# The last norm out of the mixing norm's statistics, bf16 counts, and a query bias that rides with the side information

## What the kernel must compute

```python
x = x + tanh(g_xattn[0]) * attention(layernorm(x), ctx, side)   # softmax(Q K^T / 16 + beta * side) V, 64 keys
x = x + tanh(g_ffn[0])   * experts(layernorm(x))                # a shared expert and 2 of 8 routed experts a row
x = x + tanh(g_xattn[1]) * mixing(layernorm(x), ctx)
x = x + tanh(g_ffn[1])   * (round_and_clip(layernorm(x) / step) * step @ (ternary - 1).T + bias)

def attention(n, ctx, side):
    Q = n @ Wq.T + bq; K = ctx @ Wk.T + bk; V = ctx @ Wv.T + bv
    return softmax(Q @ K.T / 16 + beta * side) @ V

def mixing(f, ctx):                                   # f: 512 x 256, ctx: 64 x 256
    h = tanh((ctx @ Ws)[None] + (f @ W)[:, None] + b)  # 512 x 64 x 256 values of tanh a sequence
    att = softmax(h @ w + mask)                        # 512 x 64
    t = att @ ctx
    return tanh(t @ Wcw) * f + tanh(t @ Wcb)           # two numbers a row: ws and bs
```

## Time and profile before

| what | us |
|---|---|
| median of 3 runs (lowest, highest) | 1095.37 (1093.33, 1097.17) |
| the profiled execution | 1098.02 |
| its span, first to last instruction | 1096.3 |
| PE, DVE, ACT, POOL busy in the span | 996.7, 748.8, 668.2, 216.5 |

### The profile page before, as it was taken

One profiled execution on the slowest core, in us unless ns is written; L12 is line 12 of the kernel. 1 busy time (PEld: TensorE's weight loads), 2 busy tenths in 40 slices (PEclk: granted clock), 3 DMA queues, 4 the chain that ended last, 5 costly groups with the idle time before them and its releaser, 6 DMA issues.

```text
span 1096.3 us, 23452 instructions
## 1 busy us (share of the span) xinstructions
PE 996.7 (91%) x8772; PEld 771.5 (70%) x8772; DVE 748.8 (68%) x2110; ACT 668.2 (61%) x966; POOL 216.5 (20%) x257
## 2 busy tenths in 40 slices
PE   6889999999999999999999999999999999966661
PEld 2568777787779999977777777777777777622220
DVE  2566788877653345644578678578588488898876
ACT  1211111111101111399999999999999999999990
POOL 1032123331250003121122121131131121310000
PEclk9859999999999999999999999999999999999895
DMA  8011101100039999876466456656665564100000
GB/s 254 25 63 58 39 30 63 44 34 15 30 104 333 336 332 341 305 246 214 160 222 229 176 197 228 202 198 204 207 217 197 186 231 155 40 16 21 1 20 19
DMA packets 114053, 164.21 MB, mean 150 GB/s; under 512 B 13235, under 2 KB 70068, under 8 KB 113940
## 3 DMA queue, kind: packets, MB, share of 16 engines
q1 hardware_dynamic: 104004, 135.57, 36.9%
q0 software_dynamic: 9936, 27.15, 6.7%
HBM read 138.69 MB, written 23.99 MB: 148 GB/s over the span
## 4 chain that ended last, share of the span: by engine, by line
PE 72%; DVE 11%; issue 7%; ACT 7%; DMA 2%; POOL 1%; SPq 0%; POOLq 0%; DVEq 0%; ACTq 0%
PE bank L1130 21%; PE bank L1313 16%; PE bank L1292 11%; PE bank L1135 6%; PE bank L1283 3%; PE bank L1172 2%; PE bank L1116 2%; PE bank L1300 2%; ACT arena L656 2%; PE bank L1187 2%; PE bank L1219 1%; PE bank L1245 1%; DMA picked<-expert_rows,found_at 1%; DVE ln_moe_stats L748 1%; DVE x L818 1%
## 5 line engine op out<-in xcount | busy, mean ns | idle before, releaser
L1130 PEld LDWEIGHTS bank<-rowsT,expert_w 128*128 128x128 f32 x2272 | 270.8, 192 | 10.3 <-issue 6.2
L1130 PE MATMUL bank<-rowsT,expert_w 128*128 128x128 f32 x2272 | 276.6, 275 | 0.5 <-DVE rowsT L938 0.5
L648 ACT ACTIVATE act<-bank 128x512 f32<-128x512 f32 x103 | 61.3, 595 | 211.9 <-PE bank L1130 115.2
L1292 PE MATMUL bank<-expert_w,act 128*128 128x256 f32 x568 | 138.6, 387 | 1.8 <-DVE rowsT L938 1.7
L573 POOL DMA_DIRECT2D expert_rows<-rows_out x71 | 42.6, 601 | 492.7 <-DVE rows_out L955 492.7
L1135 PE MATMUL bank<-normT,shared_w 128*128 128x256 f32 x512 | 126.8, 396 | 0.0
L955 DVE COPY rows_out<-bank 128x256 f32<-128x256 f32 x71 | 30.1, 425 | 141.2 <-PE bank L1292 140.5
L664 ACT ACTIVATE tanhs<-shared_w,txtT 128x512 f32<-128x512 f32 x168 | 122.0, 726 | 2.1 <-DVE shared_w L981 2.1
L1292 PEld LDWEIGHTS bank<-expert_w,act 128*128 128x128 f32 x568 | 102.2, 190 | 28.8 <-issue 15.9
L665 ACT ACTIVATE tanhs<-shared_w,txtT 128x512 f32<-128x512 f32 x168 | 122.0, 726 | 0.0
L1135 PEld LDWEIGHTS bank<-normT,shared_w 128*128 128x128 f32 x512 | 98.3, 198 | 17.3 <-issue 3.0
(11 more groups left out here) (230 smaller groups left out, 1483.8 us busy)
## 6 DMA issues: line engine op xcount, KB each, us to landing
expert_w<-in_WgT SPq DMA_DIRECT2D x71, 512.0 KB, 4.0
expert_w<-in_WuT SPq DMA_DIRECT2D x71, 512.0 KB, 5.2
expert_w<-in_WdT SPq DMA_DIRECT2D x71, 512.0 KB, 6.7
rows_in<-rows_by_expert SPq DMA_DIRECT2D x71, 128.0 KB, 5.8
expert_rows<-rows_out POOLq DMA_DIRECT2D x71, 128.0 KB, 4.3
x<-in_x SPq DMA_DIRECT2D x8, 512.0 KB, 4.2
out<-x SPq DMA_DIRECT2D x16, 256.0 KB, 2.7
score<-in_fside SPq DMA_DIRECT2D x8, 128.0 KB, 2.3
```

The lines of the kernel that those rows point to most:

```text
L648: e.activation(act[n % 2][:, :], banks[2 * (n % 2)][:, :], ACT.Tanh, scale=0.5).then_inc(s_tanh, 1)
L1130: got = e.matmul(bank[:, i * P:(i + 1) * P], w[:, at:at + P], t[:, c * P:(c + 1) * P], start=c == 0, stop=c == DC - 1)
L1292: got = e.matmul(row_bank[:, 0:D], act[n % 2][:, c * P:(c + 1) * P], w[:, at:at + D], start=c == 0, stop=c == IC - 1)
```

## The change

Three edits of the computation, and a new set of numbers for the order.

- **The last norm.** Since x' = A x + B, its mean is A mean + B and its variance A * A * var, so (x' - mean') * r' is (x - mean) * (A * r'). The kernel after takes the variance as (1 + w1) * (1 + w1) * var with w1 = g * ws * r in three small instructions (`stretch`), so `stats` and `aggr` of that norm go; `quantize` reads x and the mixing norm's mean before `apply` has run, and `apply` moves behind `quantize`. `affine` runs between POOL's power and `newton`. The two weighted sums become one of twice the width (`weigh_c`).
- **Counts.** `before`, `chosen` and a new all-ones tile are bf16.
- **Query bias.** The prologue makes `bias_q` by a weight whose 128 columns are all bq, so the bias stands in all 128 lanes, scaled; `side` adds it together with the scaling, and the product L1183 goes. `side` of the first sequence now waits for ACT's copy of `bias_q`.
- **Numbers.** `PLACES` and `LAGS` change all over; `PAIRS` goes from 2, 4, 4, 4, 4, 4, 8, 12 to 8, 4, 4, 5, 4, 4, 10, 13, which makes 166 preadd instructions of DVE's behind the last gate activation where there were 146, and 416 in all where there were 336.

```diff
-PAIRS = {0: 2, 1: 4, 2: 4, 3: 4, 4: 4, 5: 4, 6: 8, 7: 12}
+PAIRS = {0: 8, 1: 4, 2: 4, 3: 5, 4: 4, 5: 4, 6: 10, 7: 13}
-    "scalar": {"gate_act": -2.5, "soft_rho": 1, "softmax": -2, "spread": 7.5, "squash": 0.5, "tanh": 1.5, ("turn", "att"): -0.5,
+    "scalar": {"gate_act": -1, "soft_rho": 1, "softmax": -2, "spread": 7.5, "squash": -1, "tanh": 0.5, ("turn", "att"): -0.5,
...
-        return ([[("rho", b)], [], [("turn_rho", b)], [("soft_rho", b)], [("rsum", b)], [("weigh_ws", b)], [("weigh_bs", b)],
-                 [("squash", b)], [("affine", b)], [("apply", b)]] + self.norm("lin", b, False)
-                + [[("step", b)], [("quantize", b, 0)], [("quantize", b, 1)], [("add_bias", b)], [], [("turn_q", b)],
-                   [("linear", b, 0)], [("linear", b, 1)]])
+        return [[("rho", b)], [], [("turn_rho", b)], [("soft_rho", b)], [("rsum", b)], [("weigh_c", b)], [("squash", b)], [("stretch", b)],
+                [("power", "lin", b)], [("affine", b)], [("newton", "lin", b)], [("step", b)], [("quantize", b, 0)], [("quantize", b, 1)],
+                [("apply", b)], [("turn_q", b)], [("add_bias", b)], [("linear", b, 0)], [("linear", b, 1)]]
...
-                    e.tensor_scalar(score[b % 2][:, :, :], score[b % 2][:, :, :], side_w, None, ALU.mult).then_inc(s_side, 1)
+                    if b == 0:
+                        e.wait_ge(s_misc[misc["bias_q",][0]], misc["bias_q",][1])
+                    e.scalar_tensor_tensor(out=score[b % 2][:, :, :], in0=score[b % 2][:, :, :], scalar=side_w,
+                                           in1=bias_q[:, b * T:(b + 1) * T].unsqueeze(1).to_broadcast([P, ST, T]),
+                                           op0=ALU.mult, op1=ALU.add).then_inc(s_side, 1)
...
+                elif name == "weigh_c":
...
+                    chain(lambda: e.tensor_tensor(products, rho_e[:, :, :].unsqueeze(1).to_broadcast(per),
+                                                  ctx_w[:, :, b * T:(b + 1) * T].unsqueeze(2).to_broadcast(per), ALU.mult))
+                    chain(lambda: e.tensor_reduce(weighed[:, :, :], products, AX, ALU.add))
+                    linked(lambda: e.tensor_tensor(weighed[:, :, :], weighed[:, :, :],
+                                                   sm["rsum"][:, :].unsqueeze(1).to_broadcast([P, 2, ST]), ALU.mult)).then_inc(s_ws, 1)
+                    link(e.tensor_scalar(sm["gr"][:, :], ln_of("mix", b)["r"][:, :], GX1, None, ALU.mult))
+                elif name == "stretch":
...
+                    e.wait_ge(s_squash, b + 1)
+                    chain(lambda: e.tensor_tensor(w1, weighed[:, 0, :], sm["gr"][:, :], ALU.mult))
+                    chain(lambda: e.scalar_tensor_tensor(out=t, in0=w1, scalar=1.0, in1=var, op0=ALU.add, op1=ALU.mult))
+                    chain(lambda: e.scalar_tensor_tensor(out=t, in0=w1, scalar=1.0, in1=t, op0=ALU.add, op1=ALU.mult))
...
-                    for i in range(ST):
-                        for c in range(DC):
...
-                                           keysq[:, c, b * T:(b + 1) * T], start=False, stop=(i, c) == (ST - 1, DC - 1))
+                                           keysq[:, c, b * T:(b + 1) * T], start=c == 0, stop=c == DC - 1)
...
-                        got = e.matmul(bank[:, (i + 1) * E:W].rearrange("p (j e) -> p j e", e=E), ones[:, :],
+                        got = e.matmul(bank[:, (i + 1) * E:W].rearrange("p (j e) -> p j e", e=E), onesb[:, :],
```

More of the change, by code:

```diff
@@ L52 @@
-    "tensor": {"count": -1.5, "feature": -2, "linear": 2.5, "scores": -0.5, "spread": 2.5, "sum": 0.5, "text": 8,
-               ("turn", "mix"): -0.5, "weigh": -2},
+    "sync": {"load_side": -1.5, "load_x": -1.5, "narrow": -2.5},
+    "gpsimd": {("power", "att"): 1.5, "scatter": -0.5},
+    "scalar": {"gate_act": -1, "soft_rho": 1, "softmax": -2, "spread": 7.5, "squash": -1, "tanh": 0.5, ("turn", "att"): -0.5,
+               ("turn", "mix"): -1.5, "turn_e": 1.5},
+    "vector": {"add": 0.5, "add_bias": 2.5, "affine": 0.5, ("aggr", "att"): 2.5, ("aggr", "lin"): -0.5, ("aggr", "moe"): 0.5,
+               "apply": 3.5, "choice": -1.5, "convert": -20.5, "feature": 0.5, "find": 3, "gate_act": 3, "linear": 4, "narrow": 2,
+               ("newton", "att"): 2, ("newton", "lin"): -1.5, ("newton", "mix"): 1, ("newton", "moe"): 1, "place": -0.5,
+               ("power", "att"): 1.5, "preadd": -1.5, "quantize": 1, "rho": -6.5, "rsum": 1.5, "side": -3.5, "sigmoid": 1.5,
+               "softmax": 0.5, ("stats", "att"): 2.5, ("stats", "mix"): 1.5, "step": -3, "sums": 4, "text": 10.5,
+               ("turn", "moe"): -0.5, "turn_q": 1.5, "turn_rho": -3, "turn_rows": 0.5, "weigh": -1, "weigh_ws": -0.5},
@@ L54 @@
+    "tensor": {"count": -1.5, "feature": -1.5, "linear": 5.5, "logits": 0.5, "scores": -0.5, "spread": 2, "sum": 1, "text": 7,
+               ("turn", "mix"): -0.5, "turn_rho": -4, "up": 2.5, "weigh": -2},
 }
@@ L321, in build @@
         identb = sb("identb", [P, P], BF16)
[L322 removed]
+        before = sb("before", [P, P], BF16)
+        onesb = sb("onesb", [P, P], BF16)
         ones = sb("ones", [P, P])
```

113 lines of the change are left out of this document (47 added, 66 removed).

## The result

| what | before | after |
|---|---|---|
| median (lowest, highest) | 1094.35 (1092.38, 1097.17), 4 runs | 1080.0 (1078.55, 1080.64), 4 runs |
| ratio, 95% interval | | 0.9865 [0.9839, 0.9891] |
| profiled execution, span | 1098.02, 1096.3 | 1080.55, 1078.8 |
| PE, DVE, ACT, POOL busy | 996.7, 748.8, 668.2, 216.5 | 983.1, 756.8, 656.3, 217.3 |

What follows compares the result with a forecast made beforehand. Bound by a PE-DVE ring in the shared stage, PE in the routed stage, ACT in the tail, then the output chain. Shared -5.2, routed 0, tail -4.2, chain -4.1 sum to -13.5: 1081.9 us from 1095.37, range 1073 to 1091.

Steps and rivals of the forecast that it cites:

- Output chain: After the last tanh: shorter weighted sums and last norm, with `apply` behind `quantize`, give -4.1 us, bounds -3.3 and -4.5.
- Tail: From the last gate activation: ACT's shorter queue gives -6.9 us, new waits for DVE take 2.7 back: -4.2.
- Rival B: Tail: DVE holds ACT up a few more times and the 6.9 us go: 1086 us; chance 0.14.
- Routed stage: Expert tiles between shared stage and tail: no product changes and PE has no wait there; 0 us, bounds -2 and +3.
- Rival D: Routed stage: sums wait for tanh once a tile, 0.2 us in each of 60 tiles: 1095 us; chance 0.07.
- Shared ring: Shared stage's loop through PE and DVE: PE's leg, count and DVE's waits sum to -0.7 us a period, -4.2 over six.
- The count: Shared stage on PE: five bf16 instructions at 0.38 us replace the f32 ones, gain 0.65 a sequence, upper bound 1.03.
- The copy wait: Shared stage on PE: with `up` behind the logits, PE stands 0.78 us a period for ACT's copy of the second transposes.
- DVE's leg: Shared stage: DVE's waits for exp and at `narrow` shrink, 0.5 to 1.1 us a period, taken as 0.85.
- rival C: First shared periods: PE's low clock lasts one period longer, some 23 us more: 1105 us; chance 0.06.
- The first 80 us: The two sequences ahead and last router steps, outside the ring: about 2 us of work goes, 1.0 counted.
- A: Shared stage: DVE's leg never ends last, so PE alone sets a period of 32.2 us: 1074 us; chance 0.13.

Runs made afterwards that it cites:

- numbers_only: The kernel before with the new PLACES, LAGS and PAIRS alone, the output chain's own numbers kept old; ratio to before 1.0155.
- control: The kernel after, unchanged, run again on another chip; ratio to before 0.9848.
- norm_only: The kernel before with the last-norm edit alone, in the old order; ratio to before 1.0077.
- fillers: The kernel after with five constant-tile transposes, or one 128 x 512 f32 product, put in front of the logits; ratios to before 0.9848 and 0.9855.
- f32_counts: The kernel after with the counts in f32 again, the order unchanged; ratio to before 0.9932.
- up_back: The kernel after with every fourth unit's `up` in front of the shared stage's logits again; ratio to before 0.9808, in a second run 0.9801.

## Why the prediction was right, and where it wasn't

- **Output chain, -4.1: right,** 27.6 to 23.5, each part within 0.1.
- **Tail, -4.2: right,** -4.4. The two sources are now apart: PAIRS 2.6, the rest, with the gate's place in it, 1.8. The rows were read slightly wrong: 92 and 40 instructions are 46 + 80 = 126 tanh units left in the tail, not 86, and the gate's place is worth three units, not two; the instructions, and so the sum, are right. Rival B was near: in `numbers_only`, with the old output chain and its own old numbers, ACT waits 5.9 us, and nothing is gained.
- **Routed stage, 0: in its bounds,** +2.2. One period of 81.4 has a PE wait of 1.0 for `rows_out` (in `control` too), and the waits for `rowsT` from 410 to 430 us are 2.3 for 1.7. Rival D's loss of 0.2 a tile isn't there; `norm_only` shows that waits and dips can cost 4 us a period here, from the output chain's side.
- **Shared ring, -0.7 a period: wrong.** By its own steps: `row_qb` 0.62, right. The count, taken as 0.65, measures 0.90: the five bf16 instructions cost 0.13 together, where the price from the eight bf16 transposes was 0.38; my upper bound of 1.03 holds. The copy wait 0.78, right. DVE's leg, taken as 0.85, gives what is left: 34.3 - 32.9 = 1.4 at full clock (32.9 from the fillers' periods without a dip), so about 0.7. At full clock that would have been -8 over six periods. The failed step is the clock: I asked in rival C only whether the first periods' low stretch would last longer, and took 2.4 GHz from the row of a ring whose order I was changing. Seven times 1.7 (one dip counts twice) turned -8 into +4. That there are so many is the order and the chance of the period's length together.
- **The first 80 us, mis-sized.** "About 2 us of work, of which I count 1.0": it is -10.9 in the two profiled executions. 2.9 of it is the dip at the first scores, chance, and not the change. The period behind the first logits fell from 33.5 (`norm_only`) to 27.5: at half clock the products that leave cost more (the f32 counts 3.2 in `f32_counts`, for 0.9 at full clock), and the first `up` now stands behind the logits that end this stretch.
- **Logits 7 to the first routed product,** -4.3, also in that 1.0: the count, a wait of 1.54 us for the gate activation and one of two dips are gone.
- **Rivals.** A (1074) lost as a time; the full-speed period of 32.9 is near its 32.2, and `up_back` reaches 32.05. C had the clock, but in the wrong place: the first periods' granted clock went up (0.56 to 0.65), their long low stretch from 20.5 us to 17.1, and the dips came in every later period, too cheap to turn the sign.

So the total was right with two errors against each other: 8 us too much hoped of the ring, some 11 too little of the stretches around it (without the 2.9 of chance, which also brings the profiled 17.5 to 14.6, next to the 14.4 of the medians). The tail and the chain were forecast; the shared stage came out by luck.

## What to carry to other kernels

Where an order is a ring through PE, ask of each product moved not only whose wait it covers but whether the clock stays up behind it: here moving one `up` behind the logits widened the stretch in which the clock can fall, and each dip costs as much as an edit gains. A count of dips from one trace is no measure of an edit before it is seen where in the period the clock could change at all. An edit that shortens a list of steps in a plan laid out by numbers moves all its neighbours; measured without its numbers it can show the opposite sign (-4.1 us forecast, +8 measured). Parts measured alone gave -0.7, -0.25, +0.8 and, for the numbers, +1.6%, and the whole -1.4%: with such a plan parts can't be added.
